# Edge convolution of a two-layer early-fusion model: split F32R operands over both image halves instead of F32 by halves

## The reference, cut to what matters

```python
def _L0_tok_ref(x, scharr):                       # x: 8 x 3 x 256 x 256
    gray = einsum('bchw,c->bhw', x, (0.2989, 0.587, 0.114))[:, None]
    edges = conv_general_dilated(gray, scharr, (1, 1), 'SAME')   # two 3x3 filters
    return abs(edges).sum(axis=1) / 2             # 8 x 256 x 256: 256 tokens of width 256
...
h = concatenate([edge tokens, text tokens], axis=1)   # 8 x 384 x 256
h = h + attn0(layernorm(h))    # 16 heads of 16, rotary, causal, then a gelu MLP of 1024
h = h + ternary_ffn(layernorm(h))
h = h + attn1(layernorm(h))    # 16 heads of 64, 4 key heads, linear bias
h = h + experts(layernorm(h))  # 8 experts, 2 per token
```

## Time and profile before

| | |
|---|---|
| time, median of 3 runs | 1924.7 us (1924.65 to 1927.76) |
| the profiled execution | 1929.46 us, of which the span is 1927.6 us |
| SETUP and PRO, with the start of unit 0 | 0 to about 100 us |
| rest of unit 0 | to 190.9 us |
| units 1 to 4 | 190.9 to 532.6 us, 85.3 to 85.4 us each |
| mean granted clock of TensorE | 0.952 |

### The profile page before, as it was taken

The page is one execution under the profiler, slowest core; times in us unless marked ns, Lnnn a source line. Parts: engine busy times, 40 slices in busy tenths (PEclk is TensorE's granted clock), DMA queues, the critical chain, the costliest instruction groups (busy, mean ns, idle before and its releaser), DMA issues.

```text
span 1927.6 us, 33422 instructions
## 1 busy us (share of the span) xinstructions
PE 1783.2 (93%) x11132; PEld 1422.5 (74%) x11132; DVE 1231.2 (64%) x4053; ACT 964.0 (50%) x2658; POOL 544.5 (28%) x763
## 2 busy tenths in 40 slices
PE   4788999999998999899999999981999999999997
PEld 2455677786866767577777777761889998999896
DVE  6677677776867666667676777657664445444452
ACT  1355657575666756656656665630133334233431
POOL 2241433424242311111111111110425334534431
PEclk8687999999999999999999999995899999999998
DMA  6111010101101010002101110012213221222210
GB/s 208 39 36 64 1 62 1 61 9 53 38 8 58 2 34 16 20 21 73 34 2 34 34 34 26 2 42 68 86 45 121 94 73 42 82 79 66 63 40 21
DMA packets 74242, 90.99 MB, mean 47 GB/s; under 512 B 16523, under 2 KB 64310, under 8 KB 74072
## 3 DMA queue, kind: packets, MB, share of 16 engines
q1 hardware_dynamic: 61464, 67.88, 10.8%
q0 software_dynamic: 9472, 16.77, 3.1%
q10 hardware_dynamic: 3136, 4.21, 0.6%
HBM read 71.00 MB, written 25.00 MB: 50 GB/s over the span
## 4 chain that ended last, share of the span: by engine, by line
PE 74%; issue 10%; DVE 6%; POOL 2%; ACT 2%; DMA 2%; POOLq 1%; DVEq 1%; SPq 1%; ACTq 0%
PE bank L1576 17%; PE bank L1017 17%; PE bank L1591 9%; PE bank L965 6%; PE bank L1000 6%; PE bank L949 6%; PE bank L921 2%; PE bank L1176 2%; PE bank L1039 2%; PE bank L976 1%; PE bank L901 1%; DVE probs L2253 1%; PE bank L922 1%; DVE at_least L2860 1%; POOLq L3070 1%
## 5 line engine op out<-in xcount | busy, mean ns | idle before, releaser
L1699 ACT ACTIVATE probs<-probs,nmax 128x128 f32<-128x128 f32 (+2 forms) x768 | 381.0, 501 | 62.6 <-DVE nmax L2253 62.4
L965 PE MATMUL bank<-cst,probs 128*128 128x128 f32 x1536 | 235.1, 280 | 17.0 <-ACT probsT L1707 9.1
L965 PEld LDWEIGHTS bank<-cst,probs 128*128 128x128 f32 x1536 | 182.6, 143 | 65.2 <-issue 25.7
L1576 PE MATMUL bank<-xeT,gate_w 128*128 128x480 f32 x768 | 189.1, 382 | 1.6 <-issue 1.6
L1576 PE MATMUL bank<-xeT,up_w 128*128 128x480 f32 x768 | 187.8, 380 | 0.0
L2395 DVE COPY probsT<-bank 128x384 f32<-128x384 f32 x256 | 141.1, 551 | 68.3 <-PE bank L965 67.1
L1591 PE MATMUL bank<-down_w,hT 128*120 128x256 f32 x1536 | 181.3, 280 | 0.0
L1591 PEld LDWEIGHTS bank<-down_w,hT 128*120 128x120 f32 x1536 | 179.9, 181 | 0.1
L3010 DVE TENSOR_TENSOR prod<-bank,sil 128x480 f32<-128x480 f32 x128 | 84.0, 656 | 147.8 <-PE bank L1576 132.0
L3113 POOL COPY rinv<-rowsum 128x384 f32<-128x384 f32 x80 | 40.9, 511 | 485.1 <-DVE o1T L2275 292.9
L1707 ACT COPY probsT<-bank 128x384 f32<-128x384 f32 x256 | 121.7, 476 | 111.3 <-PE bank L965 102.4
(11 more groups left out here) (321 smaller groups left out, 3357.2 us busy)
## 6 DMA issues: line engine op xcount, KB each, us to landing
gate_raw<-in_L_ffn_gate_w SPq DMA_DIRECT2D x8, 1024.0 KB
up_raw<-in_L_ffn_up_w SPq DMA_DIRECT2D x8, 1024.0 KB
down_raw<-in_L_ffn_down_w SPq DMA_DIRECT2D x8, 1024.0 KB, 5.7
img<-in_x SPq DMA_DIRECT2D x8, 768.0 KB
residual_rows<-x SPq DMA_DIRECT2D x8, 384.0 KB, 2.5
residual_rows<-h_in SPq DMA_DIRECT2D x8, 384.0 KB, 3.6
xr<-residual_rows SPq DMA_DIRECT2D x8, 384.0 KB, 4.3
hr<-residual_rows SPq DMA_DIRECT2D x8, 384.0 KB, 3.6
```

What stands on the lines that cost most here:

```text
L965: last = tr(ps[bank][:, P * q:P * (q + 1)], probs[:, n % 4, SEG[t] + P * j:SEG[t] + P * (j + 1)], ident)
L1576: last = mm(ps[bank][:, 0:HALF], w[:, wp, c, P * m:P * (m + 1)], xeT[:, xp, c, HALF * hf:HALF * (hf + 1)], start=(c == 0 and k == 0), stop ...
L1699: last = f(p, p, ACT.Exp, bias=nmax[:, n % 4, t:t + 1], scale=-1.0, accum_out=rowsum[:, where, t:t + 1])
```

## The change

- **The convolution** is made per filter, not per half: a bank takes the 512 columns of both halves for one filter. Its operands are F32R (a 32-bit float of reduced precision, which needs one pass), and each is split into an upper part, rounded to F32R, and the rest: three products (upper weight by upper image, upper by lower, lower by upper) for each of three shifts, and one with the halo block. That is 10 instructions of 128 x 512 per filter and 20 per image.
- **The gray image** is split by a cast on ScalarE (gray_uppers) and a subtraction on VectorE (gray_lowers, which waits for the cast), into a tile gray_parts.
- **The halo** is a block of 18 rows, loaded by six DMAs of three rows each (two from the upper, one from the lower part per seam row), after gray_lowers. ScalarE scales it into two half blocks (halo_halves, two instructions of 18 x 256), so that one product serves both halves.
- **The absolute values**: filter 0's go from PSUM straight into h_in on ScalarE, filter 1's are taken in place in PSUM; VectorE's edges then adds them to h_in for both halves in a row.
- **The edge weights**: VectorE makes the band matrices as before, then splits them (a cast and a subtraction of 128 x 768), with some small ones more for the halo's weights. Eight small loads stand where four did.
- **Order in MID0**: on PE qk_1 moves ahead of scores(3), and the convolution's two parts move behind it, on both sides of qk_2. On VectorE take qk_1 now stands behind mlp_norm(1), both edge sums behind take qk_2, and first_norm(0) and (1) behind take_turned(7). On POOL rope(1) and rope(2) move ahead of deviation(FIRST, 0). Unit 0 and unit 6 share these lists. In PRO the whole convolution of image 1 stands behind qk_2.

The diff, cut to its core:

```diff
@@ psum_plan, order of the names on banks 6 and 7 @@
-        add(k.s1, "qk_0")
+        add(k.s1, "qk_0", "qk_1")
+        add(k.s1p, "k1_0", "q1_2")
         add(k.conv, "conv0")
-        add(k.s1p, "k1_0", "q1_2")
+        add(k.s1, "qk_2")
         add(k.conv, "conv1")
-        add(k.s1, "qk_1", "qk_2")
@@ SP, load_halo @@
-                sp.wait_ge(gray_ready, i + 1)
-                for k, row in enumerate((P - 1, 0)):
-                    for dx in range(3):
-                        sp.dma_start(halo_gray[dx:dx + 1, k, :], gray[row:row + 1, k, dx:dx + IMG]) \
-                            .then_inc(halo_loaded, 16)
+                sp.wait_ge(gray_split, i + 1)
+                if i > 0:
+                    sp.wait_ge(halo_ready, i)
+                for hf, row in enumerate((0, P - 1)):
+                    for part in range(3):
+                        q = 9 * hf + 3 * part
+                        src = gray_parts[row:row + 1, part % 2, 1 - hf, 0:IMG].bitcast(F32)
+                        shifted = bass.AP(src.tensor, src.offset, [src.ap[0], [1, 3], [1, IMG]])
+                        sp.dma_start(halo_rows[q:q + 3, :], shifted).then_inc(halo_loaded, 16)
@@ PE, convolve @@
-                for hf in halves:
...
-                    for k in range(2):
-                        o = ps[bank][:, IMG * k:IMG * (k + 1)]
-                        for dx in range(3):
-                            mm(o, band[:, k, dx, :], gray[:, hf, dx:dx + IMG], start=(dx == 0), stop=False)
-                        last = mm(o, edge_w[:, hf, k, :], halo_gray[:, 1 - hf, :], start=False, stop=True)
-                    last.then_inc(filled[bank], 1)
+                for k in kinds:
...
+                    for dx in range(3):
+                        for w, x in ((0, gray_hi), (0, gray_lo), (1, gray_hi)):
+                            mm(ps[bank][:], band[:, w, k, dx, :], x[:, :, dx:dx + IMG],
+                               start=(dx == 0 and w == 0 and x is gray_hi), stop=False)
+                    mm(ps[bank][:], edge_w[:, k, :], halo[:], start=False, stop=True).then_inc(filled[bank], 1)
@@ ACT @@
+            def halo_halves(img_no):
+                act.wait_ge(halo_loaded, at(img_no, 16 * HALO_LOADS, 16 * HALO_LOADS))
+                for hf in range(2):
+                    last = f(halo[:, hf, :], halo_rows[:], ACT.Identity, bias=0.0, scale=halo_side[:, hf:hf + 1])
+                last.then_inc(halo_ready, 1)
+
+            def gray_uppers(img_no):
+                act.wait_ge(gray_ready, at(img_no, 1, 1))
+                nc.scalar.copy(gray_hi[:, :, 1:IMG + 1], gray[:, :, 1:IMG + 1]).then_inc(gray_upper, 1)
...
+                if k == 0:
+                    if img_no[0] is not None or img_no[1] > 0:
+                        act.wait_ge(spilled, at(img_no, 32, 0))
+                    f(h_in[:, 0:2, :].rearrange("p t d -> p (t d)"), ps[bank][:], ACT.Abs).then_inc(freed[bank], 1)
+                else:
+                    f(ps[bank][:], ps[bank][:], ACT.Abs).then_inc(edge_sizes_ready, 1)
@@ DVE @@
+            def gray_lowers(c):
+                dve.wait_ge(gray_upper, at(c, 1, 1))
+                inner = slice(1, IMG + 1)
+                tt(gray_lo[:, :, inner], gray[:, :, inner], gray_hi[:, :, inner].bitcast(F32), ALU.subtract) \
+                    .then_inc(gray_split, 1)
@@ DVE, unit() for MID0 @@
                     take_turned(0)
+                    gray_lower_part()
...
                     mask_max(6)
-                    edge_sum(0)
                     mlp_norm(1)
-                    first_moments(0)
                     take_queries_keys(1)
                     mask_max(7)
                     mlp_norm(2)
                     take_queries_keys(2)
+                    edge_sum(0)
+                    edge_sum(1)
                     take_mlp()
                     take_turned(4)
-                    edge_sum(1)
                     mask_max(8)
+                    first_moments(0)
                     first_moments(1)
@@ POOL, unit() for MID0 @@
                     deviation(LN_MLP, 2)
-                    deviation(LN_FIRST, 0)
                     rope(1)
                     rope(2)
+                    deviation(LN_FIRST, 0)
                     deviation(LN_FIRST, 1)
```

150 lines of the change are left out of this document (98 added, 52 removed).

## The result

| | before | the change |
|---|---|---|
| median | 1926.2 us (1924.65 to 1928.46, 4 runs) | 1944.5 us (1939.72 to 1946.84, 4 runs) |
| ratio to before | | 1.0079, 95% interval 1.0062 to 1.0095 |
| profiled execution: time, span | 1929.46, 1927.6 us | 1939.72, 1937.9 us |

The change makes the kernel slower by 15.2 us (0.79% of 1926.2), as the ratio has it; the two medians of four runs each differ by 18.3 us (0.95%), which is the upper end of its interval. A second set of runs (e10) gave 1.0078 (1.006 to 1.0096), with medians 15.7 us apart.

A forecast was written before the change was run, and what follows sets the result against it. PE's own queue bounds the loop, a chain of waits the start. Terms: 13 (start) - 4 (unit 0) + 2.7 (units 1 to 5) + 1.4 (unit 6) + 1.3 (clock) = +14.4, on the median 1939.1 us; range 1923 to 1949.

The forecast's parts named there:

- the wait for bank 6: Units 1 to 5: qk_2 waits until VectorE takes qk_1, at +8.2 us, leaving 0.35 of 3.4 us gained.
- the clock falls in every unit: Rival: each of units 1 to 5 pays 1.3 us, 5.3 us more in all, 1944.4 us; chance 0.2.
- start, to lnA of unit 0: Start: gather +7.1 us, first norm another +5.1, image 1's convolution +0.8, together +13, bounds 9 to 16.
- unit 0: Unit 0: rope(1) no longer behind deviation(FIRST, 0) and qk_1 made early, some 4 us shorter, bounds 0 and -6.
- units 1 to 5 without the clock: Units 1 to 5: -0.35 + 0.9 = +0.55 us per unit, five times +2.7 us.
- falls of the clock in them: Units 1 to 5: the new wait causes one fall of the clock in five, +1.3 us, between 0 and 6.6.
- unit 6: Unit 6: no convolution fills PE's wait for VectorE to take qk_1; +1.4 us, between 0 and 3.
- the loop gives back what PE saves: Rival: bank 6 is free by +5.1 us, so all 3.4 us count in five units, 1917 us; chance 0.13.
- PE's price of a filter: Convolution on PE: ten products of about 231 ns, 2.5 us with the tail; 5.0 us per image instead of 8.4.
- The gray image's two steps: Units 1 to 5: VectorE's subtraction passes on 0.69 us, the wait on ScalarE about 0.2, 0.9 us per unit.
- The second image's cast: Start: image 1's subtraction waits for a cast behind ScalarE's taking of the second text product; first norm another +5.1 us.
- The start is absorbed: Rival: another chain hides the start's loss of 13 us, sum +1.4, 1926 us, no change to tell; chance 0.14.

The follow-up runs named there:

- e10: The change run again, unchanged, against the kernel before: 1943.3 us, ratio 1.0078.
- e1: The change with one line moved, VectorE taking qk_1 right behind mask_max(5), ahead of mlp_norm(0) and mlp_norm(1): 1927.1 us, ratio 0.9988.
- e5: The change with six of nine band products of each filter left out, only upper weight by upper image kept: 1945.1 us, ratio 1.0079.
- e8: As e7, with the subtraction for images 2 to 7 on POOL and not on VectorE: 1914.9 us, ratio 0.992.
- e4: The change with ScalarE's cast for image 1 ahead of the text products instead of behind them: 1939.2 us, ratio 1.0052.
- e2: The change's arithmetic in the kernel before's order on PE, sizes taken out and added ahead of mlp_norm(1): 1926.5 us, ratio 0.9995.
- e7: The change with e2's order in units 1 to 6, qk_1 early in unit 0, and the moves of e3 and e4: 1919.5 us, ratio 0.9954.
- e9: The kernel before with unit 0's lists alone in the change's order, banks kept from the other units' list: 1933.4 us, ratio 1.0028.
- e12: As e11, with unit 0's banks in the order of its own products: 1913.5 us, ratio 0.9925.
- e6: The kernel before with POOL's list alone changed, rope(1) and rope(2) ahead of deviation(FIRST, 0): 1933.0 us, ratio 1.0019.
- e11: As e8, with VectorE taking qk_1 behind mlp_norm(1) in unit 0: 1917.4 us, ratio 0.9943.
- e3: The change with image 0's cast on VectorE instead of ScalarE: 1938.2 us, ratio 1.005.

## Why the prediction was right

The forecast of +14.4 us stands beside 15.2 (18.3 between the medians), with its sign and its main mechanism, the wait for bank 6. That the sum is so near is in part luck: the start was put too high by 3 to 5 us, and the clock and unit 6 too low by 4 together. The 1944.4 of the rival "the clock falls in every unit" stands beside the median of 1944.5, but what it asks for didn't happen: two of five units had the fall. Its terms:

| term | forecast | the change's two profiles |
|---|---|---|
| start, to lnA of unit 0 | +13 | +9.5, +10.1 (+8.2 between the means of all profiles) |
| unit 0 | -4 | -4.1, -1.9 |
| units 1 to 5 without the clock | +2.7 | +2.3, +2.3 |
| falls of the clock in them | +1.3 | +3.2 (two of 1.6) |
| unit 6 | +1.4 | +3.7, +3.1 |

- **Bank 6, shown.** Free at +8.2 us, idle times of 0.7, 0.35 and 1.8 (forecast 0.7, 0.5, 2.2). e1 removes the wait by one line and brings 17 us; e5 lengthens it by the 1.4 us of work taken away. The rival "the loop gives back what PE saves" named the condition that decides, and e1 met it by what that rival said, VectorE taking qk_1 ahead of the norm.
- **PE's price of a filter.** The term was 2.5 us, with 231 ns for each of ten products. A band product took 0.26 and the one with the halo 0.42, in all 2.75. So the 0.35 us left over per unit were none, and the saving in place is 3.0 instead of 3.4. The forecast's own upper end, halo products at double cost, adds up to 5.5 us per image, which is what was measured, and not to the 6 written there.
- **The gray image's two steps** cost 0.74 us per unit against 0.9, and 0.7 to 0.8 by e8.
- **The clock.** "I take one fall in the five" was mis-sized. Two came in each profile, of 1.6 us, between the forecast and the first rival, and three in e4's. In e5, with 3.2 us of idle time in one piece, the slower matmuls were in all five units; in e1 and e2, without it, in none. The row that the 1.3 us were taken from was one draw of several: 2.37 us of idle time stand at that place of unit 6 in eight profiles, and the eight matmuls behind it took 5.02, 5.40, 5.38, 4.82 and 6.37 us in five (before, e2, e7, e9, e12) and 3.70 in three (e6, e8, e11).
- **Unit 6** was mis-sized: I counted qk_2's wait but set it against the 2.37 us of the earlier trace rows as if these overlapped, and left out that half clock follows an idle time of 4.9 us. In e1 a wait for the next norm took part of its place.
- **The start** was put too high: its three parts were +3.9, +4.5 and +1.0 where the forecast had +7.1, +5.1 and +0.8. The first, for the gather, had these steps off. ScalarE began its table load at 13.42 and not at 15.61 (-2.2). I had taken one profile's number for a fixed one: with the start of before it is 15.61, 15.65 and 13.63 in three profiles. With the change's start it is 12.91 to 13.42 in six, so the change may have a part in it (in it SP doesn't issue the halo's DMAs at the same time); that was not tested. The hash, which I had ending with the convolution at 37.0, ended at 34.1, by the table load and by its own length (10.0 us and not 10.8), and this gives nearly all of 35.3 instead of 38.5. The convolution ended even earlier than forecast, at 32.3 and not 37.2, with its second filter faster (2.39 for nine). That brought nothing, as PE then waited 1.87 us for the hash; where the second filter ran slower (e10), it was 0.9 us later at the gather. The reference was off too: of the three profiles with the start of before, the one I counted from has the earliest gather. And that the first matmuls run at half clock is read from their durations alone, as the profile's granted clock is 1.00 up to about 32 us, where six passes take 2.90 us.
- **The second image's cast** cost +4.5 (8.4 less 3.9). e3 and e4 show both waits to be the cause, one by one, and that they add up nearly: 7.2 of 8.3 us.
- **Unit 0.** The number came out in one profile and to half in the other. Its reason, that rope(1) no longer stands behind the deviation, fell with e6: POOL waited for qk_1, and the deviation ahead cost nothing. That leaves qk_1's place on PE. In the change and in e9 the rotation of rope(1) starts 11.2 to 11.3 us behind lnA and not 15.7, about 4.4 earlier, as forecast. With qk_1 late and POOL's list of the change (e2) it starts 13.4 us behind lnA, after a wait of 2.27 us, and the unit takes 83.69 us; with qk_1 early (e12) it starts at 11.3 and the unit takes 81.63. So the early rotation is shown to come from qk_1's place. How much shorter it makes the unit isn't shown as well: e9, which was to show it alone, was spoiled by the banks, the change's order took 80.5 to 82.9 us in five profiles, and the order of before stands in one (84.80). Beside the rounding the rotation took 3.74 to 3.79 us in every profile, as in the earlier trace rows, and rope(2)'s, without it, 1.68 to 1.71. That agrees with the rule on the shared port pair of the Trainium skill ("SBUF — State Buffer", section "SBUF: two separate sides"). But rope(1) came clear of the rounding in no run, so the 6 us that the forecast gave for that case were not put to the test.
- **"The start is absorbed"** was wrong: e3 and e4 each take a part of the start's loss away, and each brings 0.3% of the whole time (1.0079 to 1.005 and to 1.0052). Nor did unit 0 grow as its start came earlier (81.2 and 81.9 us in e3 and e4, 80.7 and 82.9 in the change).

## What to carry to other kernels

Before an engine's saved work is counted, ask what the next product in its list waits for, and count that from the same start: here one 0.7 us instruction, placed behind a wait for a third engine, held a bank and took back all of a saving of 3 us per unit. When the order of products changes, the buffers that alternate between them change partners with it, and the list of the engine that empties them has to move too. If a cast or a subtraction is added, put it on the engine with idle time at that place, and look what stands at the head of that engine's list at the start.

## What the runs showed of the hardware

- An idle time of 1.8 us ahead of the same matmuls was followed by slower ones (granted clock 0.7 over 5.7 us in unit 2) in two or three of five units in each of four profiles, and not in the others; one of 2.37 us in unit 6 in five of eight profiles; one of 3.2 us (e5) in all five units; one of 4.9 us in all five profiles that have it. The 1.8 us cost 1.6 us a time.
- An F32R product of 128 x 512 took 0.26 us with 128 rows of weights and 0.42 us with 18, where it was the last of a bank. Whether the 18 rows or the place before another product make it longer was not tested.
- POOL subtracts 128 x 512 floats in 1.28 us, VectorE in 0.69; where POOL idles, the slower engine is the cheaper one.
- ScalarE's row of DMA issues at the start ended between 12.91 and 15.65 us over fourteen profiles, with 15.61, 15.65 and 13.63 for the same start. A wait placed behind such a row can inherit this scatter.
- The first convolution of the kernel before, with the same instructions, had its matmuls at double duration for half of its length in one profile (to 25.65) and to its end in another (e9, to 33.0), and the gather behind it moved from 31.41 to 34.63. A stretch at the start that is read from one profile can be off by 3 us for this alone.
